# One transformer layer on one core: the turned input goes through DRAM in one store and four loads, and the second FFN input is normalised in the last attention steps

## What is computed

```python
x = x + attn(layernorm(x))          # rms_norm with gamma, qkv = xn @ w_qkv, softmax(q k^T / 8) v, @ w_out
h = layernorm(x)
p = softmax(h @ router_w); top2 = top_k(p, 2) / sum(top_k(p, 2))
x = x + (gelu(h @ w1 + b1) @ w2 + b2) * sum(top2)
```

## Time and profile before

| | |
|---|---|
| median of 3 runs | 1219.67 us |
| the profiled execution | 1217.49 us, span of its instructions 1215.7 us |
| busy share of the span | PE 97%, PE weight loads 85%, DVE 81%, ACT 72%, POOL 54% |
| mean granted TensorE clock | 0.993 |
| DMA | 71.04 MB, 121512 packets, of them 75808 under 512 bytes |
| attention, about | 95 to 985 us in regular steps |
| FFN, about | 985 us to the end |

### The profile page before, as it was taken

The page is one execution under the profiler, slowest core; times in us unless marked ns, Lnnn a source line. Parts: engine busy times, 40 slices in busy tenths (PEclk is TensorE's granted clock), DMA queues, the critical chain, the costliest instruction groups (busy, mean ns, idle before and its releaser), DMA issues.

```text
span 1215.7 us, 29007 instructions
## 1 busy us (share of the span) xinstructions
PE 1175.6 (97%) x11195; PEld 1029.0 (85%) x11195; DVE 979.7 (81%) x1737; ACT 873.5 (72%) x1897; POOL 658.5 (54%) x825
## 2 busy tenths in 40 slices
PE   8999999999999999999999999999999998799999
PEld 6778888888888888888888888888888877688788
DVE  7898889888988898889888988898889876676663
ACT  6887888788878887888788878887887871333432
POOL 5776565656565656555655665566556662222321
PEclk9999999999999999999999999999999998899999
DMA  4233112311131123111311141114111432222310
GB/s 131 64 87 72 36 36 54 88 36 36 53 88 37 36 54 88 36 36 53 88 36 36 36 105 36 37 36 105 32 41 31 103 100 55 56 61 66 85 37 35
DMA packets 121512, 71.04 MB, mean 58 GB/s; under 512 B 75808, under 2 KB 115232, under 8 KB 121376
## 3 DMA queue, kind: packets, MB, share of 16 engines
q1 hardware_dynamic: 121376, 69.19, 23.2%
HBM read 19.08 MB, written 8.39 MB: 23 GB/s over the span
## 4 chain that ended last, share of the span: by engine, by line
PE 58%; POOL 9%; DVE 9%; issue 6%; SPq 6%; ACT 4%; DMA 2%; POOLq 0%; ACTq 0%; DVEq 0%
PE ps L531 26%; PE ps L602 15%; PE ps L588 8%; PE ps L554 7%; SPq L451 6%; POOL prob L930 4%; PE ps L560 3%; ACT prob L843 2%; DVE pT_lo L1046 2%; POOL att_hi_v L950 1%; POOL attT_lo L956 1%; DVE xn L1042 1%; DMA xn<-xblocks 1%; DVE negmax L1125 1%; DVE xT_lo L1047 1%
## 5 line engine op out<-in xcount | busy, mean ns | idle before, releaser
L930 POOL TENSOR_SCALAR prob<-prob,rowinv 128x512 f32<-128x512 f32 x512 | 351.6, 702 | 279.1 <-DVE rowinv L1130 278.8
L843 ACT ACTIVATE prob<-ps,negmax 128x512 f32<-128x512 f32 x512 | 346.9, 685 | 36.9 <-DVE negmax L1125 33.2
L1046 DVE TENSOR_TENSOR pT_lo<-ps,pT_hi 128x512 fp32r<-128x512 f32 (+1 forms) x384 | 319.8, 860 | 20.3 <-ACT pT_hi L836 15.9
L1125 DVE TENSOR_REDUCE negmax<-ps 128x2 f32<-128x1024 f32 x256 | 310.4, 1213 | 1.4 <-PE ps L560 1.2
L588 PEld LDWEIGHTS ps<-identity,prob 64*128 64x128 f32 x4096 | 154.0, 138 | 71.6 <-issue 18.5
L833 ACT ACTIVATE pT_hi<-ps 128x1024 fp32r<-128x1024 f32 x128 | 131.6, 1028 | 112.6 <-issue 112.0
L588 PE MATMUL ps<-identity,prob 64*128 64x64 f32 x4096 | 178.2, 226 | 13.4 <-DVE xres L1058 10.6
L554 PE MATMUL ps<-nat 64*128 64x512 f32 x1024 | 171.4, 412 | 0.3 <-DVE nat L1047 0.3
L602 PE MATMUL ps<-pT_hi,vbuf 128*128 128x256 f32 x1024 | 165.3, 284 | 1.9 <-DVE pT_lo L1046 1.9
L602 PE MATMUL ps<-pT_lo,vbuf 128*128 128x256 f32 x1024 | 165.4, 284 | 0.0
L602 PEld LDWEIGHTS ps<-pT_hi,vbuf 128*128 128x128 f32 x1024 | 145.5, 192 | 8.0 <-DVE pT_lo L1046 2.6
(11 more groups left out here) (117 smaller groups left out, 2305.0 us busy)
## 6 DMA issues: line engine op xcount, KB each, us to landing
att_hi_v<-halves_out SPq DMA_DIRECT2D x128, 128.0 KB, 2.4
att_lo_v<-halves_out SPq DMA_DIRECT2D x128, 128.0 KB, 2.4
xn<-xblocks SPq DMA_DIRECT2D x240, 32.0 KB, 1.9
xres<-in_x SPq DMA_DIRECT2D x8, 512.0 KB, 3.6
x_scratch<-xres SPq DMA_DIRECT2D x8, 512.0 KB, 4.0
out_y<-f_o SPq DMA_DIRECT2D x15, 256.0 KB, 2.3
xin<-in_x SPq DMA_DIRECT2D x7, 512.0 KB, 4.6
wstage<-in_w SPq DMA_DIRECT2D x4, 512.0 KB, 4.0
```

Of the source, the lines that this page charges most:

```text
L843: act.activation(prob[:, n % NPROB, j * SEQ:(j + 1) * SEQ], ps[:, PS_SCORE[n % 2] + j, :], ACT.Exp, bias=negmax[:, n % 4, j:j + 1], accum_ ...
L930: return pool.tensor_scalar(dst, src, scalar, 1.0, ALU.mult, ALU.mult)
L1046: return dve.tensor_tensor(dst, full, hi, ALU.subtract)
L1125: dve.tensor_reduce(negmax[:, n % 4, :], ps[:, PS_SCORE[n % 2]:PS_SCORE[n % 2] + 2, :], AX.X, ALU.max, negate=True).then_inc(s_max, 1)
```

## The change

1. The blocks are turned in another layout (`xn_by_block`, `turn_input`), stored to DRAM in one DMA (`store_blocks`) and read back in four (`spread_input`), 1 KB rows in place of 128-byte rows. The input is loaded by four DMAs that regroup its tokens (`load_input`), and `xT` is written and read in groups of 32 columns (`by_group`).
2. The normalisation tasks of a batch begin at slot 5, not 9.
3. POOL's `input_hi` stands before the second `normalise_prob` of step 13.
4. The statistics, normalisation and turn of FFN block 1 run in slots 252 to 255 (steps 126 and 127); its store is issued at slot 255 and its four loads at slot 257, ahead of the last weight load.
5. In block 0, `route(1)` stands before the last output projection, `x2_hi(1)` behind the fifth gelu and `ffn_split(1)` behind the fourth `hidden_lo`. PE waits for three, not four, of the last output tiles before `down`.
6. FFN statistics read `xin`; the residual is loaded apart (`load_x1`) into two buffers, not three.

The diff, cut to its core:

```diff
-NEXT_LN_SLOT = 9
+NEXT_LN_SLOT = 5
+LAST_LN_SLOT = NUNIT - 4
...
-PS_ROUTER = 4
+PS_ROUTER = 2
...
+    blocks_dram = nc.dram_tensor("blocks_scratch", (2 * B - 1, P, TT, D), F32, kind="Internal").ap()
...
-        f_x1 = [xin[:, :, :], prob[:, 2, :].rearrange("p (t d) -> p t d", t=TT), xres[:, :, :]]
-        xn_turned = xn[:, :, :].rearrange("p t d -> p (t d)").rearrange("p (k q) -> p k q", k=KT)
+        f_x1 = [prob[:, 2, :].rearrange("p (t d) -> p t d", t=TT), xres[:, :, :]]
+        xn_by_block = xn[:, :, :].rearrange("p t d -> p (t d)").rearrange(
+            "p (c k t j) -> p c k t j", c=P // QUAD, k=KT, t=TT)
+        xn_turned = xn[:, :, :].rearrange("p t d -> p (t d)").rearrange("p (g k q) -> p k g q", g=P // QUAD, k=KT)
...
+            def load_input(m):
+
+                source = x_v[m] if m < B else x1_dram[m - B]
+                by_group = source.rearrange("(t i) g d -> g i t d", t=TT)
+                for g in range(P // QUAD):
+                    sp.dma_start(xin[g * QUAD:(g + 1) * QUAD], by_group[g]).then_inc(s_x, 16)
+
+            def store_blocks(m):
+                sp.wait_ge(s_blocks, 2 * m)
+                sp.dma_start(blocks_dram[m - 1], xblocks[:, :, :]).then_inc(s_stored, 16)
+
             def spread_input(m):
 
-                sp.wait_ge(s_blocks, 2 * m)
-                for g in range(P // QUAD):
-                    for c in range(P // QUAD):
-                        sp.dma_start(turned_rows(c, g), block_rows(g, c)).then_inc(s_spread, 16)
+
+                sp.wait_ge(s_stored, 16 * m)
+                by_column = blocks_dram[m - 1].rearrange("(g j) c n -> c j g n", g=P // QUAD)
+                for c in range(P // QUAD):
+                    sp.dma_start(xn[c * QUAD:(c + 1) * QUAD], by_column[c]).then_inc(s_spread, 16)
...
                 if slot == UP_SLOT + 1:
+                    sp.wait_ge(s_xn, B + 1)
+                    load_input(B + 2)
+                    spread_input(B + 1)
                     sp.wait_ge(s_pt, 2 * NUNIT - 2)
-                    load_x1(1)
-                if rel == 24 and b + 2 < B:
+                    load_x1(0)
...
+                        sp.wait_ge(s_xn, b + 1)
+                    if b + 2 >= B:
+                        sp.wait_ge(s_x1, 16 * (b + 3 - B))
+                    load_input(b + 2)
...
                 if rel == 23 and 0 <= b < B:
                     spread_input(b + 1)
+                if slot == NUNIT - 1:
+                    store_blocks(B + 1)
...
                     sp.dma_start(xres[:, :, :], x_v[b]).then_inc(s_xres, 16)
+                    store_blocks(b + 1)
...
             spread_logits(0)
-            spread_input(B + 1)
...
-            load_x1(2)
+            load_x1(1)
             for c in range(B):
                 if c + 1 < B:
                     spread_logits(c + 1)
                 if c + 2 < B:
+                    store_blocks(B + c + 2)
+                    sp.wait_ge(s_base, c + 1)
+                    load_x1(c + 2)
+                if c + 3 < B:
+                    load_input(B + c + 3)
+                if c + 2 < B:
                     spread_input(B + c + 2)
                 store_out(c, 0)
                 store_out(c, 1)
...
             for c in range(B):
                 for f in range(TAIL_UPS if c == 0 else 0, FT):
                     up(c, f)
+                if c + 1 < B:
+                    route(c + 1)
                 if c == 0:
                     for block_of_out in last_out:
-                        if block_of_out == last_out[-1]:
-                            pe.wait_ge(s_flt, 1)
                         aux(LAST_STEP + 1, *block_of_out)
                     wait_weight_split(pe, N_CHUNKS - 1)
-                    pe.wait_ge(s_aux, len(aux_index))
-                if 1 <= c < B - 1:
-                    route(c + 1)
+                    pe.wait_ge(s_aux, len(aux_index) - 1)
                 down(c, 0)
                 down(c, 1)
-                if c == 0:
-                    route(1)
                 down(c, 2)
...
-                for f in range(TAIL_UPS if c == 0 else 0, FT):
+                first = TAIL_UPS if c == 0 else 0
+                for f in range(first, FT):
                     gelu(c * FT + f)
-                    if f == TT - 1 and 1 <= c < B - 1:
+                    if f == max(first, TT - 1) and c + 1 < B:
                         x2_hi(c + 1)
...
                     router_exp(0)
-                    x2_hi(1)
...
+                if task == (B + 1, 1):
+                    powers(B + 2)
...
                     attention_out(step // 2 - 2)
+                if split_step(step):
+                    input_hi(split_step(step))
                 if 0 <= 2 * step < NUNIT:
                     normalise_prob(2 * step)
...
-                if split_step(step):
-                    input_hi(split_step(step))
...
-                    if c == 0 and f == len(HIDDEN_SLOTS):
-                        powers(B + 2)
...
+            def normalise_by_block(t):
+
+                return normalise(xn_by_block[:, :, :, t, :],
+                                 xin[:, t, :].rearrange("p (k c j) -> p c k j", k=KT, c=P // QUAD), t)
...
-
-                dve.transpose(xblocks[:, k], xn[:, :, k * P:(k + 1) * P]).then_inc(s_blocks, 1)
+            def wait_input(m):
+                dve.wait_ge(s_x, 16 * (P // QUAD) * m)
+
+            def turn_input(half):
+
+                places = slice(2 * half, 2 * half + 2)
+                dve.transpose(xblocks[:, places, :].rearrange("p c n -> p (c n)"),
+                              xn[:, places, :].rearrange("p c n -> p (c n)")).then_inc(s_blocks, 1)
...
-                    if slot == HIDDEN_SLOTS[0]:
-                        for t in range(TT):
-                            ffn_stats(1, t)
...
+                    if b > B and step < 2:
+                        ffn_stats(b - B, 2 * step)
+                        ffn_stats(b - B, 2 * step + 1)
+                    elif b > B and step == 2:
+                        ffn_normalise(b - B)
+                    elif b > B:
+                        turn_input(0)
+                        turn_input(1)
...
-                    if 1 <= c < B - 1 and f == TT - 1:
+                    if f == TT - 1 and c + 1 < B:
                         ffn_split(c + 1)
+                        if c == 0:
+                            turn_logits(0)
...
-                    ffn_split(1)
```

66 lines of the change are left out of this document (28 added, 38 removed).

## The result

The changed kernel takes 1189.61 us (median of 4 runs, 1188.78 to 1189.91). The kernel before took 1218.89 us beside it, so the ratio is 0.976, with a 95% interval of 0.974 to 0.978. The profiled execution took 1189.91 us, with a span of 1188.1. The forecast was 1193, the range 1186 to 1203. Its three terms hold to within 1.4 us, but the cause that it gave for the third is not what the runs show.

A forecast was written before the change was run, and what follows sets the result against it. PE's own work bounds the kernel (busy 120.75 of 122 us per batch), so only its gaps and slow stretches can be won. 9.8 + 6.0 + 10.6 = 26.4 us from 1217.5 gives 1191.1, for the median 1193; range 1186 to 1203.

The forecast's parts named there:

- Term A: Split step 13 of attention batches 0 to 6: PE's wait behind `xres` goes, 1.4 us each, 9.8 us.
- the even trade: Last attention steps: early statistics use up the 1.5 us DVE no longer waits at the eighth split; neither counted.
- Term B: FFN blocks 2 to 6: ACT's waits for `x2_hi` go, input chain 8.9 us for 13.2; 6.0 us won.
- Term C: Transition to the FFN: five waits and low clock, 17.3 us, less the costs of three points, leaves 10.6 us won.
- the signs that the prediction listed: Trace: `xres` wait gone, steps about 7.5 us, ACT waits under 3, `route(1)` not waiting, four SP issues in some 2.5.
- Point 1: Step 127: DVE's normalisation and turn precede the `pT_lo` that values of step 128 need; costs PE 2.5 us.
- Point 2: FFN block 0: last weight chunk loads behind store and eight loads, delaying ACT's gelus; costs 1.5 plus 1.0 us.
- Point 3: FFN block 1: first gelus wait for router's exponentials, `x2_hi(2)` comes late; costs 1.7 us, bounds 0 and 4.
- The rule weighed against this part: Way through DRAM: fixed DMA part of about 2 us paid twice, 8.0 us with issues; sum would not change.
- Rival 1: Transition gives back its gain: Point 1 to Point 3 cost 13.6 us, Term C is 3.7, time 1200; chance 0.17.
- Rivals 2 and 3: DRAM way no shorter (13 us, time 1202, chance 0.07); split step not freed, DVE full (1201, chance 0.07).
- Rival 4: Split step: late loads stall POOL's probabilities, up to 1 us per batch per microsecond after 478.4; slower, chance 0.04.

The follow-up runs named there:

- E2: Changed kernel with POOL's `input_hi` put back at the end of the split step; 1200.38 us, ratio 0.985.
- E1: Kernel before, only `input_hi` moved ahead of the second `normalise_prob` of the split step, 16 copies kept; 1216.08 us, ratio 0.997.
- E5: Changed kernel with 16 copies between SBUF tiles where the store stands, in place of store and four loads; 1220.06 us, ratio 1.000.
- E9: E3's kernel with block 1's statistics and their power also put back where the kernel before has them; 1191.29 us, ratio 0.977.
- E4: Kernel before, `x2_hi` and the split of the next FFN input two gelus later in blocks 1 to 5; 1210.08 us, ratio 0.993.
- E6: E3's kernel with 16 copies between SBUF tiles in place of store and loads; 1215.67 us, ratio 0.998.
- E3: Changed kernel with block 1's normalisation, turn, store, loads, split and router product back in FFN block 0, statistics still early; 1187.94 us, ratio 0.975.
- E10: Changed kernel with, in the FFN, the four loads of turned blocks issued ahead of the four input loads; 1186.27 us, ratio 0.973.
- E12: E10's kernel with block 1's normalisation and turn at the end of step 128, its DMAs, `x2_hi(1)` and router product moved too; 1182.43 us, ratio 0.971.

## Why the prediction was right, and where its reason was wrong

**Term A: right in size and cause.** 10.4 us by the traces, 10.8 by E2, where the sum had 9.8. Of the two conditions, the order on POOL is shown by E2, the early data by E1. What the prediction priced as landing time is more a matter of SP's queue: E5's copies start three slots earlier and free the split step too, but their 11.06 us of issues hold up a `regroup` in the step before. The eighth split gave another 1.5 us between the values of steps 125 and 126 (6.35 us after, 7.82 before); the next step, with the statistics in it, takes back 1.1 (8.43 after, 7.36 before, 7.76 in E9 without the statistics), close to the even trade that the prediction made of the two.

**Term B: right, a little small.** 7.3 us against 6.0. The `up` phases of blocks 2 to 6 have become 7.3 us shorter (62.4 to 55.1 together); 6.5 of that were the waits, and the rest lies in the matmuls themselves. E4 shows by its time that moving `x2_hi` and the split wins as much. The transport is worth 5.5 us of it (E6 against E3); with 16 copies the five waits are 4.6 us in E6, where they were 6.5, and what shortened them there was not tried apart. But the chain was put at 8.9 us and is longer: from the store at 1016.10 to `x2_hi(2)` at 1026.92 it is 10.8. The store was faster than the 4.0 us taken, 3.0 (in the batches it lands after 5.0, where three slots hide it); the loads slower than 2.4, at 4.6, because the input loads are issued ahead of them, which I had counted as hidden. The later `x2_hi` wait 0.35 us at most, so the error stayed without effect there; in block 1 it cost what E10 wins back.

**Term C: right in size (9.8 against 10.6), wrong in cause.** The step that failed is the sentence "Both disappear if block 1's input is made beforehand". E3 makes it as late as before and is as fast, so most of both waits goes without that. Two parts of the change do it, and each has its wait. One is the statistics, 1.4 us on DVE and 2.0 with what follows them, ahead of the hidden parts; the prediction set them against the eighth split and did "count neither". They set most of the wait of 2.78 us: 0.66 in E3, 2.43 in E9. So the sentence that put it to normalisation and turn alone failed too. The other is the transport, which sets the 3.09 us of `route(1)`: 3.00 with copies in E6, 1.38 and 1.45 without in E3 and E9. Whether an early normalisation without early statistics would also remove the first wait was not run. The table shows the way: from the last values to block 1's `down` it is 59.0 us before, 53.5 in E6 (early statistics, with the smaller edits around them, and still copies), 48.6 in E3 (the transport as well) and 45.6 in the changed kernel. Of the 10.4 us from the kernel before to E3, E9 gives 2.6 to the statistics and E6 4.8 to the transport; 3.0 are left for the smaller edits of the list of changes or for the parts together, and stay open. The last 3.0, for the input made beforehand, are paid with 2.4 to 3.9 in steps 125 to 129. Nearly all the signs that the prediction listed came out (the waits behind ACT are 3.0 us where it has under 3, and `route(1)` waits 0.33), but none of them could tell these parts from each other.

**The three points of C**, by their sizes:
1. Point 1 was 2.5 us with bounds 1 and 4.6; it is 3.7 in this execution: from the values of step 127 to those of 128 it is 10.5 us, and 6.8 in the kernel before. In E10, with the same lists up to there, it is 9.3 and the point just 2.5: both wait as long for `xres` (2.54 and 2.55 us), and in the changed kernel the clock is 0.66 at 977 to 982, behind that wait, in E10 it is 1.00 at 979 to 984. DVE's timeline of step 127 in the changed kernel has the normalisation between the two durations of the earlier trace rows, and the turn as there:
```profile
973.96 2.11 DVE L1067 TENSOR_SCALAR xn<-xin,ln_mv,ln_scale 128x256 f32<-128x256 f32 x4
976.10 1.30 DVE L1117 STREAM_TRANSPOSE xblocks<-xn 128x512 f32<-128x512 f32 x2
```
2. Point 2 was 2.5 us and is near nothing in this execution: the weight chunk is issued at 982.61, ACT waits 1.83 us for it as it did before (1.80), and `up` 4 to 7 take 5.95 us to the start of `route(1)`, where it was 5.73 to the output projection. In E10's execution, with the same lists, ACT waits 4.58 us for the chunk, and from `route(0)` to the end of `up` 7 it is 8.0 us, where the changed kernel has 6.9 and the kernel before 6.7. So the point lies between 0.2 and 1.3 us. The store was faster and the issues shorter (1.73 us for four where 2.5 were counted). E5 shows that the mechanism is real: with 16 copies in that place it costs 7.5 us.
3. Point 3 was 1.7 us with an upper bound of 4 and is some 5: `up` of block 1 takes 16.2 us (1016.78 to 1033.02), where the later blocks take 10.9. The waits of 0.55 and 2.43 us are the start of it, the clock of 0.85 behind them most of the rest. E10 confirms the cause that the prediction named, `x2_hi(2)` behind its loads: with the loads first, 4.2 of the 5.3 us go.

The three made 6.7 in the sum and 9.2 in the trace. What was won before them is then 9.8 + 9.2 = 19.0 us where the sum had 17.3; the early statistics and the eighth split were not in that. So the sum came out by errors that nearly cancel, and that term C came out in size is luck.

**The rule weighed against this part.** The Trainium skill (DMA: Bandwidth & Descriptors, "Anatomy of one DMA — SWDGE (gpsimd) path") says that a DMA has a fixed part of about 2 us. It says so of DMAs that GpSimd issues, and here SP issues them. By its formula I estimated 3.2 us for the store and 2.3 for a load, a fixed part for each of the two. The store's 3.0 us in the FFN come close, its 5.0 in the batches do not; a load takes 3.0 in E10, and 4.6 in the crowd of the changed kernel. The landing of 4.0 us that I called in agreement is that of 512 KB, set against 128 and 32 KB, so it does not show that DRAM is the reason. Neither decides here. What E5 and E6 show to be the price of the copies is the queue: 16 issues are 11 us during which SP issues nothing else. The Trainium skill (Perfetto Trace Analysis, "What 'DMA-bound' means") names the issuing engine's sequencer as a bound of its own, seen as a track that is solid with DMAs; in E5 the track is solid for 11 us at a time and free after, and that was enough.

**The rivals.** Rival 1 (the transition gives back) came two thirds of the way: 9.2 us of its 13.6. Rivals 2 and 3 did not come about. Rival 4's price was wrong: it said that POOL held up by late data would cost up to a microsecond for each one from a landing at 478.4 on. In E1 the data land at 480.2 and the step still shrinks by 0.5 us. The probabilities have slack there, which the timeline did not show and a look at the consumer, PE's next transposes, would have.

**Left open.** E5's place for the copies is not the only one; copies on another engine's queue, or behind the `regroup` with `input_hi` ahead, were not tried in the changed kernel. E10's order with E3's late normalisation was not run either, so what E12's place is worth is known against step 127 only (3.8 us by the medians, E12 against E10, 2.4 by the pieces of the trace that its edit can reach), and E12 moved the DMAs, `x2_hi(1)` and `route(1)` along with it.

## What to carry over

Price a group of DMAs by the time that its issues take on their queue, and list what stands behind them there: one store and four loads won 28 us over 16 copies put where the store stands (E3 against E6), much of it by leaving the queue free. When a change has several parts that could each remove the same wait, price each part with the others absent; a wait that disappears in the trace is not shown to have disappeared by the part that was meant to remove it. And order loads by who waits first: two groups of DMAs exchanged on one queue gave 3.3 us by the medians and 2.8 by the trace.

## What was not expected of the hardware

A low clock and a wait can stand for each other. Between the values of steps 126 and 127 the changed kernel waits 1.49 us for `pT_lo` at the full clock (1.00 at 960 to 970); E3 waits 0.18 us there, because the matmuls before it ran slower, in a stretch of granted clock 0.89:
```profile
950.00:960.00 10.00, 10.00 (x101) 9.03 (x100) 8.44 (x15) 8.51 (x21) 9.74 (x12) 1.00 0.47 120
960.00:970.00 10.00, 7.85 (x90) 6.94 (x91) 9.88 (x18) 8.31 (x19) 8.93 (x9) 0.89 0.27 62
...
971.74 0.51 PE L623 MATMUL ps<-pT_hi,vbuf 128*128 128x256 f32 x2 [0.18 <-DVE pT_lo L1073]
```
Both take the same time between the values of the two steps, 8.43 us (962.20 to 970.63) and 8.47 (963.27 to 971.74), and DVE is busy for 9.82 and 9.88 of the 10 us. E12 and E10 repeat the pair: 1.48 us of waiting at 1.00 and 8.43 us, 0.19 at 0.81 and 8.47. So in these steps the low clock costs nothing, because DVE's chain is the bound, and a shorter list of waits is no gain by itself.

A load from DRAM of 128 KB was issued in 0.43 to 0.57 us (1.73 to 2.27 for four), a copy of 32 KB between SBUF tiles in 0.69 (11.06 for 16), so the queue takes 1.2 to 1.6 times as long for a quarter of the bytes.
